# A decoder layer on one core: the last norm's scale at the final addition, tile registers read ahead, and 23 products that nobody reads

## The reference

```
x = x + attn(layernorm(x))                 # 16 heads, causal, Wq Wk Wv Wo with biases
x = x + xattn(layernorm(x), ctx, mask)     # 16 heads over 375 context rows
x = x + ffn(layernorm(x))
```

```
x = rms_norm(h, norm_w);  scores = softmax(x @ Wg.T);  rw, sel = top_k(scores, 2)
# rows sorted by expert; q (shared), k, v, f per expert; g = log_sigmoid(f) / 8
o = gsa_chunk(q, k, v, 1 - exp(g), g)      # slot states carried along the rows
out = sum over the two experts of rw * o
return rms_norm(out, gnorm_w) @ Wo.T       # rms_norm(y, w) = y * rsqrt(mean(y*y) + eps) * w
```

## Time and profile before

| | us |
|---|---|
| timed runs | 409.22, 407.26, 406.85 |
| profiled execution | 406.22 |
| its span, first to last instruction | 404.4 |
| TensorE busy | 378.9 |
| VectorE busy | 303.9 |
| ScalarE busy | 283.1 |
| GpSimd busy | 136.1 |

### The profile page before, as it was taken

How to read it: one execution, slowest core, us unless ns; L and a number is a source line. 1 busy time by engine, 2 the same in 40 slices (tenths; PEclk the granted TensorE clock), 3 DMA queues, 4 the chain that set the end, 5 groups by cost and what they waited for, 6 DMA issues and landing times.

```text
span 404.4 us, 11298 instructions
## 1 busy us (share of the span) xinstructions
PE 378.9 (94%) x3803; PEld 288.7 (71%) x3803; DVE 303.9 (75%) x1175; ACT 283.1 (70%) x758; POOL 136.1 (34%) x193
## 2 busy tenths in 40 slices
PE   7898999999998999899967999999999999999994
PEld 5775777787775777677755556665667888889883
DVE  2999997979979888755934986984656878786662
ACT  4134869697985979899954677778684775667561
POOL 3504224030745705330040871442033342443320
PEclk9999999999999999999997999999999999999998
DMA  6978952645553211310011234537234022222101
GB/s 188 205 216 298 304 179 70 204 128 154 142 185 119 46 40 41 99 36 39 2 46 41 72 131 159 192 144 238 81 133 161 8 76 70 62 68 68 36 24 34
DMA packets 23207, 45.87 MB, mean 113 GB/s; under 512 B 2792, under 2 KB 14792, under 8 KB 23152
## 3 DMA queue, kind: packets, MB, share of 16 engines
q1 hardware_dynamic: 21104, 37.82, 30.3%
q0 software_dynamic: 2048, 7.34, 6.1%
HBM read 26.80 MB, written 18.35 MB: 112 GB/s over the span
## 4 chain that ended last, share of the span: by engine, by line
PE 63%; DVE 16%; ACT 11%; issue 4%; DMA 3%; another core or an unknown queue 1%; POOL 1%; SPq 0%; DVEq 0%; ACTq 0%
PE ps L857 46%; PE ps L860 16%; ACT sc L1597 4%; DVE scs L1271 3%; DVE scs L1278 3%; ACT pT L1605 3%; DMA kv<-kd_d,idk 1%; DMA wqk<-in_watt 1%; DVE qkT L1228 1%; DVE kd L1454 0%; ACT u L1662 0%; DVE xn L1217 0%; ACT u L1660 0%; ACT u L1664 0%
## 5 line engine op out<-in xcount | busy, mean ns | idle before, releaser
L1597 ACT ACTIVATE sc<-sc,nm 112x375 f32<-112x375 f32 x128 | 76.4, 615 | 3.2 <-DVE nm L1261 2.8
L1261 DVE CUSTOM_DVE_ANT_0 sc<-ps,mkb 112x375 f32<-112x375 f32 x128 | 64.8, 542 | 15.9 <-PE ps L857 15.5
L857 PE MATMUL ps<-wm,xsT 128*128 x168 | 59.9, 494 | 2.0 <-DVE eti L1383 0.8
L860 PE MATMUL ps<-cst,sc 112*125 112x112 f32 x384 | 56.8, 283 | 4.0 <-ACT oT L1616 3.3
L860 PEld LDWEIGHTS ps<-cst,sc 112*125 112x125 f32 x384 | 48.3, 189 | 16.6 <-issue 6.2
L1605 ACT ACTIVATE pT<-ps 125x448 f32<-125x448 f32 x96 | 51.8, 550 | 3.7 <-remote 2.0
L857 PEld LDWEIGHTS ps<-wm,xsT 128*128 128x128 f32 x168 | 29.8, 190 | 22.1 <-issue 20.5
L1271 DVE CUSTOM_DVE_ANT_0 scs<-ps,cst 112x112 f32<-112x112 f32 x128 | 28.8, 267 | 3.7 <-PE ps L857 3.7
L1591 ACT ACTIVATE pT<-ps 112x448 f32<-112x448 f32 x32 | 16.9, 540 | 20.6 <-PE ps L860 20.2
L1849 POOL TENSOR_TENSOR qg<-okb,dc 112x256 f32<-112x256 f32 x16 | 11.9, 741 | 53.8 <-ACT okb L1703 53.8
L857 PE MATMUL ps<-cxT,cqT 32*112 32x375 f32 x256 | 28.8, 518 | 0.6 <-issue 0.6
(11 more groups left out here) (231 smaller groups left out, 931.6 us busy)
## 6 DMA issues: line engine op xcount, KB each, us to landing
kd_d<-kd SPq DMA_DIRECT2D x21, 384.0 KB, 2.6
xs_d<-xs SPq DMA_DIRECT2D x8, 896.0 KB, 7.0
wm<-in_wmoe SPq DMA_DIRECT2D x8, 768.0 KB, 4.6
cxp<-in_ctx SPq DMA_DIRECT2D x8, 420.4 KB
cxT<-in_ctxT SPq DMA_DIRECT2D x32, 93.8 KB, 3.4
xs<-xs_d SPq DMA_DIRECT2D x21, 128.0 KB, 2.1
mki<-in_mask SPq DMA_DIRECT2D x8, 164.1 KB, 5.9
out<-xbo SPq DMA_DIRECT2D x8, 112.0 KB
```

What stands on the lines that cost most here:

```text
L857: return e.matmul(o, l, r, start=start, stop=stop)
L860: return e.transpose(o, i, ident[0:n, 0:n])
L1261: e.tensor_tensor_reduce(sc[:, m % RS, j, :], ps[0:S, bk, 0:NK], mkb[:, b % 2, :], 1.0, 3e38, ALU.add, ALU.min, nm[:, m % RS, j:j + 1]).th ...
L1597: e.activation(sc[:, n % RS, j, :], sc[:, n % RS, j, :], ACT.Exp, bias=nm[:, n % RS, j:j + 1], scale=-1.0).then_inc(a_ex, 1)
```

## The change

Four things are changed, and the planner's table of ranks with them.

1. `fn` becomes a plain copy of the combined rows, and `fs` reads that copy. The scale enters in `fin`: product times scale plus x, in one VectorE instruction. gnorm_w is multiplied into `wom` by two GpSimd instructions (`foldw`), and the broadcast load of gnorm_w (and norm_w with it) is dropped.
2. SyncE has one register for each tile. It reads the first two of a group before it waits for the scatters, and each other one right behind the transfer two tiles ahead of it.
3. Twenty-three 128 x 128 products of the identity with itself go into eleven places of TensorE's order (`WARM`: planned time, number). Their result is read by nobody.
4. `BIAS` is replaced. Of it one line is shown.

```
+WARM = ((10.36, 3), (15.85, 4), (29.36, 2), (30.99, 1), (31.75, 4), (33.99, 2), (35.26, 1), (35.80, 2), (46.76, 1), (201.74, 2), (207.59, 1), )
...
+    "T": {"G": 794.3, "R": -136.2, "Sc": -536.7, "Ss": -790.7, "at": 256.6, "cb": 1217.3, "cnt": -327.5,
...
+        taken = (0.215 * WARM[stage[1]][1],) * 2 if stage[0] == "warm" else COST[eng][kind(stage)]
+        self.parts[eng, stage] = [taken, rank + BIAS[eng].get(kind(stage), 0), needs, at, len(self.parts)]
...
+        for i, (t, n) in enumerate(WARM):
+            add("T", ("warm", i), 0.2 * n, 4000, release=("T", ("warm", i)), at=t)
...
+        add("P", ("foldw", 0), 0.7, 150, [("S", ("later", NE // 2)), ("P", ("foldq", 0))])
...
-            add("A", ("fs", b), 1.2, r - 40, [("T", ("cb", b))])
-            add("V", ("fn", b), 0.5, r - 40, [("A", ("fs", b))])
+            add("A", ("fs", b), 1.2, r - 20, [("V", ("fn", b))])
+            add("V", ("fn", b), 0.5, r - 40, [("T", ("cb", b)), ("T", ("fT", b - 2)), ("A", ("fs", b - 2))])
...
-            add("V", ("fin", b), 0.45, r - 40, [("T", ("fo", b))])
+            add("V", ("fin", b), 0.45, r - 40, [("T", ("fo", b)), ("A", ("fs", b))])
...
+            rows_at = [e.alloc_register(f"row{t}") for t in range(NT)]
...
-                    e.dma_start(rw_sb[:, 3:4, :].rearrange("p a n -> p (a n)"), rows[1024:1280].partition_broadcast(S)
-                                ).then_inc(l_late, 16)
...
+                        e.load(rows_at[t:t + 2], eti[0:1, 0, t:t + 2])
                         for i in range(RY):
                             e.wait_ge(d_sc[i], 32 * len(range(i, LISTS[g][0], RY)))
                     if t >= RX:
                         e.wait_ge(t_xT, t - RX + 1)
-                    e.load(first, eti[0:1, 0, t:t + 1])
-                    row = e.snap(first, min_val=0, max_val=NE * CAP - 128)
+                    row = e.snap(rows_at[t], min_val=0, max_val=NE * CAP - 128)
                     e.dma_start(xs[:, t % RX, :], xs_d[bass.ds(row, 128), :]).then_inc(d_xs[t % RX], 16)
+                    if t + 2 < NT and TG[t + 2] == g:
+                        e.load(rows_at[t + 2:t + 3], eti[0:1, 0, t + 2:t + 3])
...
+                    if before[0][0] != "warm":
+                        e.wait_ge(*freed(before))
+                if what == "warm":
+                    for _ in range(WARM[b][1]):
+                        mm(ps[:, bk, 0:128], ident, ident)
...
-                            e.wait_ge(l_wm[0], 80)
+                            e.wait_ge(p_fo, 2)
...
-                        e.wait_ge(a_fs, 3 * t + 3)
-                        e.scalar_tensor_tensor(fin[:, r, :], ps[0:S, slot["cb", t][0], 0:256], fr[:, t, 2:3], rw_sb[:, 3, :],
-                                               ALU.mult, ALU.mult).then_inc(v_fn, 1)
+                        e.wait_ge(t_cb, NB + t + 1)
+                        if t >= 2:
+                            e.wait_ge(a_fs, 3 * t - 5)
+                        e.tensor_copy(fin[:, r, :], ps[0:S, slot["cb", t][0], 0:256]).then_inc(v_fn, 1)
                     elif what == "fin":
                         e.wait_ge(t_fo2, NB + t + 1)
-                        e.tensor_tensor(x2[:, t, :], x2[:, t, :], ps[0:S, slot["fo", t][0], 0:256], ALU.add).then_inc(v_fin, 1)
+                        e.wait_ge(a_fs, 3 * t + 3)
+                        e.scalar_tensor_tensor(x2[:, t, :], ps[0:S, slot["fo", t][0], 0:256], fr[:, t, 2:3], x2[:, t, :],
+                                               ALU.mult, ALU.add).then_inc(v_fin, 1)
...
-                        e.wait_ge(t_cb, NB + t + 1)
-                        e.activation(jnk2[:, :], ps[0:S, slot["cb", t][0], 0:256], ACT.Square, accum_out=fr[:, t, 0:1]
+                        e.wait_ge(v_fn, NB + t + 1)
+                        e.activation(jnk2[:, :], fin[:, r, :], ACT.Square, accum_out=fr[:, t, 0:1]
...
+                elif what == "foldw":
+                    e.wait_ge(l_bqk, 16)
+                    e.wait_ge(l_wm[0], 80)
+                    e.tensor_scalar(wom[:, 0, :], wom[:, 0, :], gwc[:, 0:1], 1.0, ALU.mult, ALU.mult).then_inc(p_fo, 1)
+                    e.tensor_scalar(wom[:, 1, :], wom[:, 1, :], gwc[:, 1:2], 1.0, ALU.mult, ALU.mult).then_inc(p_fo, 1)
```

More of the change, by code:

```diff
@@ L107 @@
         "qgf": (0.74, 0.71), "scatter": (2.35, 2.3), "set": (1.73, 1.7), "stats0": (0.87, 0.87),
-        "stats1": (0.91, 0.88), "stats2": (0.84, 0.84), "xn0": (0.75, 0.73), "xn1": (0.76, 0.73)},
-    "S": {"late": (2.4, 2.4), "gx": (0.8, 0.8), "zero": (0.45, 0.45), "later": (0.7, 0.7), "kd": (0.35, 0.35), "out": (0.3, 0.3), "ldmask": (0.75, 0.75), "ldctx": (0.35, 0.35), "ldctxT": (1.8, 1.8)},
+        "stats1": (0.91, 0.88), "stats2": (0.84, 0.84), "xn0": (0.75, 0.73), "xn1": (0.76, 0.73), "foldw": (0.7, 0.7)},
@@ new lines @@
+    "A": {"cpc": 5192.8, "cross_q": 308.1, "dec": 356.1, "dre": -2767.3, "e": -648.9, "es": 612.4,
+          "exc": 539.1, "fT": 1448.5, "fs": 384.1, "kTx": -4593.4, "oTc": 489.9, "oTs": -1698.1, "onT1": 4041,
+          "ones": -12.8, "q": -1261.4, "qTx": 518.3, "qe": 10151, "qgT": -1562.1, "rwe": 109.8, "siT": -903.4,
+          "sig": 7103.8, "sp": 190.1, "x": 1849, "xnT0": 23.4, "xps": 2233.9, "yT": -212.9},
+    "P": {"fold": 10.2, "foldq": -768.4, "foldw": -163.1, "gk": -5426.3, "mkb": -160, "qg": -60.8,
+          "qgf": -1138.6, "scatter": -981.9, "set": -115.6, "stats0": 417.9, "stats1": 182.6, "stats2": -89.4,
+          "xn0": -53.3, "xn1": 155},
@@ L203, in add @@
             needs.append((eng, p))
-        self.parts[eng, stage] = [COST[eng][kind(stage)], rank + BIAS[eng].get(kind(stage), 0), needs, at, len(self.parts)]
+        taken = (0.215 * WARM[stage[1]][1],) * 2 if stage[0] == "warm" else COST[eng][kind(stage)]
+        self.parts[eng, stage] = [taken, rank + BIAS[eng].get(kind(stage), 0), needs, at, len(self.parts)]
         if release:
@@ L755, in _ @@
         def _(e):
-            first = e.alloc_register("first_row")
+            rows_at = [e.alloc_register(f"row{t}") for t in range(NT)]
             def load_mask(b):
@@ L866, in _ @@
                 for before in plan.held.get(stage, ()):
-                    e.wait_ge(*freed(before))
-                if what == "xnT":
+                    if before[0][0] != "warm":
[3 more added lines that the diff above has]
+                        mm(ps[:, bk, 0:128], ident, ident)
+                elif what == "xnT":
                     if (k, b) == (0, 0):
```

36 lines of the change are left out of this document (13 added, 23 removed), and 24 rows, old and new, of tables (BIAS, COST).

## The result

The changed kernel is slower: 413.51 us (median of four runs, 412.63 to 414.80) against 407.25 for the kernel before on the same chip, a ratio of 1.0155 with a 95% interval of 1.0111 to 1.0198. Forecast were 405.0 and a range up to 408.2. The profiled execution took 414.08 us with a span of 412.3, against 406.22 and 404.4. Executions over 1.5% above the fastest of their kernel are left out of the ratios, though not out of the medians given.

A forecast was written before the change was run, and what follows sets the result against it. The prediction took TensorE to bound the kernel nearly everywhere, busy 378.9 of 404.4 us. Sum: 406.22 - 2.0 (tail) + 0.15 (products) = 404.4 profiled, 405.0 as a median of runs; 8-in-10 range 400.8 to 408.2.

The forecast's parts named there:

- change the order from about 240 us on in many small swaps: TensorE's queue, from about 240 us: swaps worth 0 where TensorE is full, bounded by 1 us either way.
- Part 1, the tail: Last batch's end: scale moved to the final addition, cb 1.74 us earlier; 2.0 us gained, bounds 0 and 2.6.
- rival D: Tail worth nothing because the last scan chain sets cb's time: 407.0 us; chance 0.13.
- the seven other batches: 0: Same scale edit in the other batches: TensorE is full there, so shorter VectorE and ScalarE waits buy 0.
- Part 2, the reads: SyncE's 21 register reads ahead of tile transfers: 0 gained, 1.4 us at most.
- rival F: SyncE's reads ahead are on the path: 1.4 us less, 403.6; chance 0.04.
- Part 3, the products: 23 unread TensorE products, twenty in the first 48 us: cost 0.15 us, mostly hidden in pauses.
- The bound of 5.1: Most the 23 unread products could cost, in us, if all were paid for at about 0.22 each.
- There the trace of before has nothing to give: Clock gain from the products: none, since the granted clock was full in each slice but the dip and the last.
- B: TensorE's clock dip at 211 to 218 us goes, thanks to products in the pause: 2.0 us less, 403.0; chance 0.22.
- C: TensorE's unexplained pause ahead of 211 us goes too, as a timing accident: 4.1 + 2.0 less, 398.9; chance 0.11.
- E: Four scatters in a row stall TensorE near 120 us: 406.9 with the smaller pause, 411.3 with the larger; chance 0.08.

## Why the prediction was wrong, by its steps

**The step that failed** is the order. The prediction wrote of the new numbers that they "change the order from about 240 us on in many small swaps", worth 0 and bounded by 1 us, and of GpSimd that it is busy for 34% of the span. Both sentences priced an engine by its idle time. The swaps ahead of 240 us were read only for the scatters and the products. In them the table put GpSimd's mask ahead of its bias addition and five scalings behind it, and that lock cost 5.3 to 7.9 us of span in the four profiles that have it (after; without products; in the kernel before; with the table alone), counted against before from VectorE's last bias addition for queries and keys to the fifth scatter: 3.6 to 4.0 of pause, the rest mostly low clock. Without this term the sum would have been 1.4 us off: 0.9978 is 406.4 on the chip of the first comparison, where 405.0 was forecast. The first set of scatters, with its 1.3 us, is still in that.

**Part 1, the tail,** forecast at 2.0, gave 2.2 from the first gather to the end. TensorE and VectorE at the end:

```profile
404.68 1.03 PE L864 MATMUL ps<-oo,wc 112*112 112x256 f32 x4
405.54 1.89 PE L864 MATMUL ps<-wom,fT 128*112 128x256 f32 x8
407.27 0.36 PE L867 MATMUL ps<-cst,fin 112*128 112x112 f32 x2
408.23 1.09 PE L864 MATMUL ps<-wom,fT 128*112 128x256 f32 x4 [0.60 <-ACT fT L1752]
```

```profile
409.36 0.48 DVE L1555 SCALAR_TENSOR_TENSOR xbo<-ps,fr,xbo 112x256 f32<-112x256 f32 x1 [1.40 <-PE ps L864]
```

From the end of the last `oo,wc` (405.71) to that of the addition (409.84) 4.1 us pass, where 4.3 were forecast, with two output products in the pause of the earlier trace rows, as drawn. VectorE's copy took 0.42, the value taken. In 395.4 to 405.7 TensorE is busy for 10.21 of 10.30 us, so rival D (the scan's chain sets it) is out. But "the seven other batches: 0" holds only in the new order. Alone the edit loses 1.8%. The traces point at the copy, a new wait at the head of ScalarE's queue (11.1 us of idle time in the kernel with the old table), and what is queued behind it was not asked; no run takes this wait away alone.

**Part 2, the reads:** 0 was right, and no gain of rival F's 1.4 us shows (1.0018, and the lower end of its interval, 0.9977, is 0.9 us). Fifteen of the reads now take 0.28, the three first ones of a group, two rows each, 0.67 in the middle:

```profile
L840 SPq TENSOR_LOAD <-eti x3: 468/670/840, 224.6 to 249.4; - x3
```

and the 42 transposes have no idle time left (0.5 in the earlier trace rows). The 1.3 us that the prediction quotes from the Trainium skill (Runtime: NRT & Kernel Launch, the preamble breakdown) is there the time of register loads from HBM. The reads here take a tile in SBUF, so their 0.27 does not contradict it.

**Part 3, the products,** forecast at 0.15, cost more: 2 us alone (0.4 to 3.5), about 0.7% of the changed kernel by two ratios whose intervals overlap. The bound of 5.1 holds, the choice near its lower end does not. "There the trace of before has nothing to give" was read from one lucky execution: the reads-alone profile has a low clock at 35 to 45 us, and the mean clock of 25 timed executions of before on one chip ran from 0.979 to 0.989, the profiled one having 0.989. That the products earn something in such executions is not shown: alone, in the eight that count, they had 0.978 to 0.990.

**The first 12 us** hold some 1.1 us of the profiled difference, and that is most likely chance. TensorE passes its first 16 query and key products at one of two paces. After, then in the kernel with GpSimd's two instructions moved (so far the code of before), then without products:

```profile
7.07 3.73 PE L864 MATMUL ps<-xnT,wqk 128*128 128x112 f32 x16 [0.49 <-ACT xnT L1591]
```

```profile
7.00 3.73 PE L861 MATMUL ps<-xnT,wqk 128*128 128x112 f32 x16 [0.49 <-ACT xnT L1581]
```

```profile
6.48 2.01 PE L864 MATMUL ps<-xnT,wqk 128*128 128x112 f32 x16 [0.49 <-ACT xnT L1590]
```

Of 16 profiles six had the slow pace, and that of before the fast one. In the second of these kernels, whose code and order are those of before up to there, the ninth of VectorE's bias additions for queries and keys came at 57.52, in before at 56.40. So a sum made against that one execution starts from a lucky one. Of the four profiles in the order of before and without products it has the earliest first scatter: 116.54, against 117.66, 118.15 and 120.49.

**The rivals.** B is out: the stretch that answers to the earlier trace rows is granted 0.52. The two products did not stand in the pause either. They wait for ScalarE's `oT`, which frees their bank and which the pause itself holds up, and come behind it (a product counts as two rows):

```profile
222.15 1.10 PE L864 MATMUL ps<-cst 128*128 128x128 f32 x4 [3.31 <-ACT oT L1630]
```

```profile
222.00:229.00 7.00, 5.67 (x65) 4.75 (x66) 1.83 (x7) 3.74 (x10) 0.00 (x0) 0.52 0.20 57
```

C did not happen: the wait of 4.10 recurs with 4.14. Whether it is an accident stays open. Splitting the third set cut it to 1.27 in one profile, and on another chip it was absent in both profiles, one of them unsplit. E had the right side, and its mechanism is there in small. The first set, now four in a row, has no unknown wait in the changed kernel, but idle pieces of 0.34, 0.47 and 0.45 between TensorE's products at 122 to 124 us. The set costs 1.3 us where E's small form has 1.9, and that is the lesser part of the loss. No rival named GpSimd's scalings. The 0.05 for slower was too small for a change that replaces the order of every engine.

## What to carry to other kernels

When an order moves work on GpSimd, look in the trace of before at every VectorE instruction with two inputs in SBUF beside it, and for durations above the median of their kind: an engine that is hardly busy can still hold another. A table that was made for one form of a stage belongs to that form; price table and edit together and each alone. An instruction that waits for a late load or a new producer is priced by what stands behind it in its queue. And one profile of before is one execution of it: take more than one before reading that a stretch has no idle time or low clock to win.

## What the runs showed of the hardware

A VectorE instruction with both inputs in SBUF was held until GpSimd's whole run of back-to-back instructions was over: 4.94 us for the rest of one and five more, 2.32 for the rest and two, 2.05 for the rest of one and one more. The Trainium skill (SBUF — State Buffer, "Who interferes with whom") says that such an instruction contends with a GpSimd instruction that reads SBUF, that the pair of ports is an exclusive lock, and that the one that starts second fully blocks; one with at most one SBUF input, outside certain modes, does not contend. The rows agree in kind. They go further in length: the page speaks of one instruction, and here six passed. Read beforehand with the diff of GpSimd's order, it would have been the rival that was missing. When the lock lets go between two scalings stays open: at 135.92 in the kernel before it did so at the first change of instruction, and GpSimd's next one took 1.07 in place of 0.90.

Four scatters in a row on GpSimd went, in the fourteen profiles of all chips but the last, with waits of ScalarE and VectorE for products that TensorE has started 3 us before; they end 0.9 to 1.1 us behind the last scatter. With two scalings between the pairs the long one was 1.27 in place of 4.1 in one kernel, and the shorter one (1.90) stayed. In the two profiles from the last chip there is none of them, with four in a row as well. Why TensorE's completions are late, and why not on that chip, was not found.

Pauses of TensorE of 2.79 us (reads alone), 3.28 (before, the old dip) and 3.55 to 4.01 (the four profiles with the lock) were each followed by a stretch of some 3 to 10 us at a granted clock of 0.50, and so was one of 1.44 (table alone, at 214 us). One of 0.96 was not. The length of a pause alone did not tell.
